# Square roots on ScalarE and reciprocals on VectorE in two node stages of a four-layer graph network

## The reference

```python
def _layernorm(x, axis=-1, eps=1e-05):
    m = jnp.mean(x, axis=axis, keepdims=True)
    v = jnp.var(x, axis=axis, keepdims=True)
    return (x - m) / jnp.sqrt(v + eps)
...
x = _layernorm(x + _L0_gnn_ref(x, ...), axis=-1)
x = _layernorm(x + _L1_gnn_ref(x, ...), axis=-1)
x = _layernorm(x + _L2_gnn_ref(x, ...), axis=-1)
x = _layernorm(x + _L3_gnn_ref(x, ...), axis=-1)
```

```python
def _eq_ln(x, w0, b0, w1):
    s, v = _split(x)
    s = s - s.mean(axis=1, keepdims=True)
    s = s * jax.lax.rsqrt(jnp.square(s).mean(axis=1, keepdims=True) + EPS) * w0 + b0
    v = v * jax.lax.rsqrt(jnp.square(v).mean(axis=(1, 2), keepdims=True) + EPS) * w1[None, :, None]
    return (s, v)
...
src_s = s @ msrc_ws
src_v = jnp.einsum('nud,uk->nkd', v, msrc_wv)
dst_s = s @ mdst_ws + mdst_bs
dst_v = jnp.einsum('nud,uk->nkd', v, mdst_wv)
```

## Time and profile before

| | us |
|---|---|
| median of three runs | 8783.5 |
| lowest and highest | 8773.5, 8791.46 |
| the profiled execution, its own time | 8718.24 |
| its span, from the first to the last instruction | 8716.4 |

### The profile page before, as it was taken

The page is one execution under the profiler, slowest core; times in us unless marked ns, Lnnn a source line. Parts: engine busy times, 40 slices in busy tenths (PEclk is TensorE's granted clock), DMA queues, the critical chain, the costliest instruction groups (busy, mean ns, idle before and its releaser), DMA issues. The chain is left out here.

```text
span 8716.4 us, 182003 instructions
## 1 busy us (share of the span) xinstructions
PE 6567.3 (75%) x41992; PEld 5838.5 (67%) x41992; DVE 6227.6 (71%) x20668; ACT 4108.6 (47%) x9608; POOL 5093.1 (58%) x4620
## 2 busy tenths in 40 slices
PE   3667777774557888888998666899865679999555
PEld 3455666664447777777888666788755569998554
DVE  4667888885548888885665667566588877775787
ACT  1334555552224444444444667444366654444444
POOL 4668888884435444444554777555466644443777
PEclk9887888885559999999999888899978889999665
DMA  6872333337873333333444566445455544443555
GB/s 133 182 173 79 89 89 88 90 85 145 164 155 92 99 96 99 99 98 102 125 126 114 181 190 192 120 123 125 110 169 166 170 129 120 119 120 106 154 162 155
DMA packets 910393, 1118.45 MB, mean 128 GB/s; under 512 B 458518, under 2 KB 546422, under 8 KB 910032
## 3 DMA queue, kind: packets, MB, share of 16 engines
q1 hardware_dynamic: 728032, 812.69, 33.4%
q0 software_dynamic: 182144, 303.64, 14.7%
HBM read 650.35 MB, written 465.65 MB: 128 GB/s over the span
## 5 line engine op out<-in xcount | busy, mean ns | idle before, releaser
L451 POOL DMA_INDIRECT erow<-e_rows,edge_idx x1176 | 1247.3, 1061 | 1229.6 <-issue 1137.3
L671 POOL DMA_INDIRECT agg<-seg_rows,edge_idx x1568 | 1554.3, 991 | 656.4 <-issue 483.2
L720 POOL TENSOR_TENSOR stats<-stats,power 128x8 f32<-128x8 f32 (+1 forms) x588 | 751.8, 1279 | 866.1 <-DVE xo L712 444.4
L400 PE MATMUL banks<-w_all,xt 128*128 128x128 f32 (+1 forms) x2352 | 546.2, 369 | 795.7 <-DVE y_more L945 259.5
L400 PEld LDWEIGHTS banks<-w_all,xt 128*128 128x128 f32 x2352 | 429.3, 248 | 879.8 <-issue 872.2
L486 PEld LDWEIGHTS banks<-seg,mid 128*128 128x128 f32 x7840 | 931.9, 194 | 15.1
L486 PE MATMUL banks<-seg,mid 128*128 128x128 f32 x7840 | 933.4, 277 | 0.0
L534 ACT ACTIVATE mid_t<-banks 128x512 f32<-128x512 f32 x980 | 585.1, 597 | 315.3 <-PE banks L486 311.7
L403 PE MATMUL banks<-w_all,xt 128*128 128x128 f32 x3528 | 657.7, 339 | 0.0
L403 PEld LDWEIGHTS banks<-w_all,xt 128*128 128x128 f32 x3528 | 617.5, 254 | 0.0
L498 PE MATMUL banks<-w_all,mid_t 128*128 128x161 f32 (+1 forms) x2352 | 583.9, 330 | 2.8 <-ACT res L539 2.8
(11 more groups left out here) (276 smaller groups left out, 18225.2 us busy)
## 6 DMA issues: line engine op xcount, KB each, us to landing
x_rows<-xo SPq DMA_DIRECT2D x294, 324.0 KB, 2.6
xin<-x_rows SPq DMA_DIRECT2D x294, 324.0 KB
e_rows<-ets SPq DMA_DIRECT2D x294, 322.0 KB
dst_row<-in_dst_flat SPq DMA_DIRECT2D x294, 256.0 KB
xin<-in_x SPq DMA_DIRECT2D x196, 324.0 KB, 7.1
seg_rows<-res SPq DMA_DIRECT2D x196, 322.0 KB, 2.6
seg_rows<-res SPq DMA_DIRECT2D x98, 384.0 KB, 2.3
seg_rows<-res SPq DMA_DIRECT2D x98, 338.0 KB, 6.6
```

The costliest lines, as they stand in the source:

```text
L400: pe.matmul(flat[:, to + k * cols:to + (k + 1) * cols], of[:, k * P:(k + 1) * P], W(w_s), start=True, stop=True)
L451: pool.indirect_dma_start(erow[s.quad][:, t, 0:EROW], None, table, bass.IndirectOffsetOnAxis(idx[s.slot][:, t:t + 1], 0),).then_inc(rows_i ...
L671: pool.indirect_dma_start(agg[s.quad][:, t, 0:SUM_COLS[layer]], None, seg_rows[layer], bass.IndirectOffsetOnAxis(idx[s.slot][:, t:t + 1], ...
L720: pool.tensor_tensor(st[:, at + n:at + 2 * n], st[:, at:at + n], power[:, 0:n], ALU.pow) \
```

## The change

In the table stage ScalarE takes the square root of the eight values (a new entry with delay 0 at the head of its list), so its `front` has delay 1 and its `back` delay 2. VectorE takes the reciprocals of the eight values at the head of `scale`. GpSimd keeps the scatters alone.

In the first node layer ScalarE takes the square root of the four values of chunk t - 1, as the last entry of its list. VectorE takes their reciprocals and makes the bias of chunk t - 2 at the head of its list (`flipped_bias`), then does `combine` of t - 1, then `before` of t; until now `before` was first. GpSimd keeps the gathers alone. The other node layers and `node_first` are as they were. The value is 1/sqrt(v) as before, by another road.

```diff
+        def square_root(act, s, at, n, done, steps, sig, later=0):
+
+            st = stats[s.quad]
+            act.wait_ge(done.sem, done.after((s.g + 1) * steps - later))
+            act.activation(st[:, at + n:at + 2 * n], st[:, at:at + n], ACT.Sqrt).then_inc(sig.sem, 1)
+
+        def flipped_bias(dve, s):
+
+            st = stats[s.quad]
+            dve.wait_ge(root2_sb.sem, root2_sb.after(s.g + 1))
+            dve.reciprocal(st[:, 36:40], st[:, 36:40]).then_inc(flip_step.sem, 1)
+            dve.wait_ge(flip_step.sem, flip_step.after(s.g + 1))
+            dve.scalar_tensor_tensor(st[:, 40:44], pairs(st, 24, 0), -1.0, st[:, 36:40], ALU.mult, ALU.mult) \
+                .then_inc(bias_sb.sem, 1)
...
# node_layer, ScalarE
+                        if layer == 1:
+                            stages.append((lambda s: square_root(act, s, 32, TILES, sum_step, sum_steps, root2_sb), 1))
...
# node_layer, GpSimd
-                    pipeline(pool, chunks, [
-                        (lambda s: gather_sums(pool, s, layer, sum_step, sum_steps), 0),
-                        (lambda s: root(pool, s, 32, TILES, sum_step, sum_steps, root2_sb), 2)])
+                    gather = (lambda s: gather_sums(pool, s, layer, sum_step, sum_steps), 0)
+                    if layer == 1:
+                        pipeline(pool, chunks, [gather])
+                    else:
+                        pipeline(pool, chunks, [
+                            gather, (lambda s: root(pool, s, 32, TILES, sum_step, sum_steps, root2_sb), 2)])
...
# node_layer, VectorE
-                    if with_e:
+                    if layer == 2:
                         pipeline(dve, chunks, [(before, 0), (lambda s: final_bias(dve, s), 2), (combine, 1)])
+                    elif layer == 1:
+                        pipeline(dve, chunks, [(lambda s: flipped_bias(dve, s), 2), (combine, 1), (before, 0)])
                     else:
                         pipeline(dve, chunks, [(combine, 1), (lambda s: final_bias(dve, s), 2), (before, 0)])
...
# node_pre, VectorE, head of scale
+                        k = chain.did(dve.reciprocal(st[:, 40:48], st[:, 40:48]).then_inc(chain.sem, 1))
+                        dve.wait_ge(chain.sem, chain.after(k))
                         k = chain.did(dve.scalar_tensor_tensor(st[:, 52:56], pairs(st, 24, 0), -1.0, st[:, 40:44],
                                                                ALU.mult, ALU.mult).then_inc(chain.sem, 1))
...
# node_pre, GpSimd
-                    pipeline(pool, chunks, [
-                        (lambda s: place_rows(pool, s, where, (0, 1)), 0),
-                        (lambda s: root(pool, s, 32, 2 * TILES, pre_step, pre_steps, root_sb), 0)])
+                    pipeline(pool, chunks, [(lambda s: place_rows(pool, s, where, (0, 1)), 0)])
...
# node_pre, ScalarE
-                    pipeline(act, chunks, [(front, 0), (back, 1)])
+                    pipeline(act, chunks, [
+                        (lambda s: square_root(act, s, 32, 2 * TILES, pre_step, pre_steps, root_sb), 0), (front, 1), (back, 2)])
```

More of the change, by code:

```diff
@@ L272, in gnn_kernel @@
         root_sb, root2_sb = signal("root_sb"), signal("root2_sb")
-        bias_sb, norm_sb = signal("bias_sb"), signal("norm_sb")
+        bias_sb, norm_sb, flip_step = signal("bias_sb"), signal("norm_sb"), signal("flip_step")
         logit_mm, logit_sb = signal("logit_mm"), signal("logit_sb")
@@ L979, in node_layer @@
                 gate_sb.passed(chunks)
+            else:
+                flip_step.passed(chunks)
             for sig in (*node_in, *idx_in, *rows_in):
@@ L993, in node_pre @@
         def node_pre():
-            pre_steps, scale_steps = 2 * TILES + 4, 5
+            pre_steps, scale_steps = 2 * TILES + 4, 6
             with ExitStack() as own, nc.Block() as block:
```

## The result

The changed kernel takes 8655.6 us (median of four runs, 8651.5 to 8674.1), the kernel before 8779.5 us beside it. The ratio is 0.9861, 95% interval 0.9843 to 0.9879: that is 106 to 138 us less. The forecast was 8652 us, 4 us away. That is closer than its terms deserve: the term of the table stage was some 30 us too high, and the one of the node layer some 10 us too low by its rows.

The account below looks back on a forecast made before the run. The prediction took loops of waits through GpSimd's queue, where the root alternates with scatters and gathers, to bound both stages. Terms 46 + 88 - 3 = 131 us off the median gave 8652 us, range 8585 to 8760.

Parts of the forecast that it names:

- the term of the table stage: Table stage: pace falls from 5.37 to 4.90 us per chunk, 46 us less, bounds 0 and 78.
- the one of the node layer: First node layer: pace falls from 6.96 to 6.05 us per chunk, 88 us less, bounds -52 and +142.
- all of the 208 us in `load_place`: Table stage: SyncE's 208 us of standing until scatters have landed would vanish once the root leaves GpSimd.
- Term (c): Table stage, SyncE: stores stand ahead of a load that could go; (4.5 + 1.0 + 7.2)/3 = 4.2 us per chunk.
- the 2.2 us for the low clock: Table stage: with PE at its lower clock the products come about 2.2 us later, making 4.9 us per chunk.
- The square root on ScalarE in the table stage: Table stage: needs 3.5 us per iteration, so it hides, with some 2.9 us of slack at 4.9 us.
- The loop through GpSimd's queue: First node layer: `combine`, root, gather, `before`, `combine` take 13.94 us over two iterations, 6.97 us each, setting the old pace.
- The two new loops: First node layer: VectorE with the square root, 5.5 us; through PE's products and ScalarE, 5.3 us high clock, 7.5 low.
- the 0.83 that I carried over: First node layer: PE's granted clock of 0.83, low level in 34% of the time, used for the 6.05 us pace.
- The table loads: ScalarE: square roots in two stages need two more activation table loads, 1.28 us each, 3 us; six in all.
- The rival in which they fall inside the loops: ScalarE changes tables twice per chunk in the loops, adding 2.57 us; slower, 8842 us; chance 0.07.
- The rival in which only the node layer gains: Table stage stays at 5.37 us because transfers are its limit; 8698 us; chance 0.15.

Follow-up runs that it names:

- e3: The kernel before, unchanged, profiled a second time; ratio 0.9994 against itself, in a group of runs where the kernel before had 8839.5 us.
- e4: The changed kernel, profiled a second time: 8715.3 us, ratio 0.9866 to the kernel before.
- e13: The changed kernel with the table stage's stores at delay 6 instead of 5: 8584.7 us, ratio 0.9831 to the kernel before.
- e8: The kernel before with only the first node layer's square root on ScalarE and reciprocal on VectorE, old order: ratio 0.9913.
- e7: The kernel before with only VectorE's order changed in the first node layer (`before` last), root still on GpSimd: ratio 1.0012.
- e10: The changed kernel with one more table-stage store, 160 KB per chunk, read by nobody, on another chip: 8614.6 us, pace 5.43 us per chunk.
- e1: The kernel before with only the table stage changed, node layer as before: ratio 0.9978.
- e5: The changed kernel storing one of four rows per partition of the destination table, 240 KB per chunk less: table stage pace 4.93 us per chunk.

## Why the prediction came out

**The table stage** was forecast at 46 us less and gave about 12 by the stage's rows on one chip, 10 to 29 by timed runs. The step that failed is the one that let all of the 208 us in `load_place` go. The forecast had the scatters go out more than an iteration earlier once GpSimd was free. But they hang on the load of row numbers, which waits until the scatters of its buffer have landed, and that loop has hardly any slack: of the 22.9 us of a turn in e3 and the 22.6 in e4, 0.4 and 0.75 lie between landing and next load. The wait for scatters fell from 219 to 146 us there and did not vanish.

Term (c), the new queueing on SyncE, is real as a wait (82 to 179 us) but was wrong in its size and its reason. It took the tables to be ready 4.5 us after the scaling of the next chunk, from one turn of the earlier trace rows; in that same trace the median is 6.4 us, and only 3 of 97 turns are as short. With the 2.2 us for the low clock its own sum is (4.5 + 1.0 + 7.2 + 2.2)/3 = 5.0 us and not 4.9. And the tables do not come later because `back` has a higher delay: `front` and `back` wait for the same scaling and the same products as they did, and the median of the same interval is 6.6 us in the changed kernel (7.1 in e3, 6.9 in e4). That the stores wait longer because the scatters hold SyncE less is argued from the order of the code; no run shows it. Taking the queueing out by one number in the store's delay gave 5.02 us, some 0.3 us less by the timed runs.

**The square root on ScalarE in the table stage** hides, as forecast: VectorE waited 1.8 us for it. Only in e13, where the loads are no longer late, does this wait appear: 88 us, 58 times.

**The node layer** was forecast at 88 us less and gave 97 and 100 by its rows. The loop through GpSimd's queue, 13.94 us for two iterations, was the right reading: e8 shows that moving the root alone takes 0.8 us off (0.96 against e7 of the same group), and e7 that the order alone takes nothing. That `before` behind `combine` is worth 0.1 to 0.2 us once the root is away wasn't in the sum. The two new loops were both found. At the high clock the pace is 5.8 us in the turn shown, against 5.5: the bias block and the gap before L963 take 0.58 us instead of 0.40, and `combine` 4.78 us instead of 4.71. At the low clock the turn shown is 6.8 us, against 7.5, since the granted clock rose within it, from 0.50 between 5115.70 and 5118.50 to 0.79 from there to 5119.93: its products were with ScalarE 4.2 us after they began, not 4.8. The granted clock was 0.92, not the 0.83 that I carried over, so fewer turns were slow. These nearly cancel, 5.95 us against 6.05; the forecast's own formula, with 0.92, 5.81 and 6.83 in it, gives 5.95.

**The table loads** are six, as the forecast had it. The rival in which they fall inside the loops is out. What spoke against it was a rule of the Trainium skill ("ScalarE: Activation LUTs", section "Table sets: the hidden batching unit"): copy and identity are in every set. The trace agrees: L727 has 196 square roots and two loads, one for each of the two stages.

**The sum** was 131 us and 124 were measured, because one term was some 30 us too high, and the other some 10 too low by its rows and more by timed runs. The rival in which only the node layer gains, 8698 us, described the table stage better than the forecast did, though its reason, transfers as the limit, doesn't fit e10 and e13. That the total came within 4 us is luck in part: the rows of the two stages and the table loads add up to some 106 us, and the rest of the 124 lies in no stage that was pinned down.

## What to carry to other kernels

A slow small operation in an engine's queue costs more than its own time when it waits there for a late result and what stands behind it feeds the same loop: add up the loop through the queue and divide by the iterations that it spans. When a wait of hundreds of microseconds is to vanish, walk once round the loop of the thing waited for (load, use, landing, number of buffers), since it may be nearly as long as the loop that is removed. Read an interval from many turns before it goes into a sum; here one turn gave 4.5 us where the median was 6.4. After such a change, look at the in-order queue of transfers again; here one step more of delay for the stores brought some 26 to 31 us, and the moved root 10 to 29 in that stage.

## What the runs showed of the hardware

A DMA share of 0.94 was not a full DMA system. The same stage moved 206 GB/s at 0.96 with one more store. In the first node layer 218 GB/s went through at 0.75. The share is the time that packets took, and that time was not fixed by their size: in the table stage a packet of 1745 bytes on average took 130 ns before the change and 150 after it, and one of 1623 bytes 122 ns in e10.

Four indirect scatters had landed 14.5 us after the first was issued, whether they were issued within 6.7 us (e3) or within 5.0 (e4).

The same kernel differed from one group of runs to the next: the kernel before has medians of 8779.5, 8839.5, 8715.4 and 8726.3 us in the four groups. The chip is not the whole reason, since the second and the third of these were taken on the same one. Part of it lies in the stages that store and scatter much. `edge_softmax`, which no experiment touches, took 679 to 690 us in some profiles and 712 to 731 us in others, on that one chip too (718 to 731 in e1 to e4, 679 to 686 in e5 to e8). So a stage of one profile may be compared with another profile only when an untouched stage agrees.
